# The order of products in the grapher, and mixing stages written out with the root last on ScalarE

## What is computed

```python
h = jnp.concatenate([h, xj], axis=1)
h = gelu(_bn(_pw(h, gc_w, gc_b), ...))          # gc
h = _bn(_pw(h, fc2_w, fc2_b), ...)              # fc2
x = x + ls1 * h                                 # x1
f = gelu(_bn(_pw(x, ffn_w1, ffn_b1), ...))      # ffn1, 64 -> 256 channels
f = _bn(_pw(f, ffn_w2, ffn_b2), ...)            # ffn2, 256 -> 64
x = x + ls2 * f                                 # x2; then relu, 2x2 max pool
```

```python
y = jnp.einsum('bchw,oc->bohw', u_k, conv_w) + conv_b[None, :, None, None]
mu = mean(y over channels); var = mean((y - mu) ** 2 over channels)
t = (y - mu) / jnp.sqrt(var + 1e-5) * ln_w + ln_b; relu(t)
```

## Time and profile before

| | |
|---|---|
| median of 3 runs | 9370.02 us (9359.23 to 9374.55) |
| the profiled execution | 9378.68 us, its span 9376.8 us |
| PE busy in the span | 6280.3 us (67%) |
| DVE (VectorE) busy | 5327.1 us (57%) |
| ACT (ScalarE) busy | 4362.6 us (47%) |
| mean granted TensorE clock | 0.872 |

### The profile page before, as it was taken

The page is one execution under the profiler, slowest core; times in us unless marked ns, Lnnn a source line. Parts: engine busy times, 40 slices in busy tenths (PEclk is TensorE's granted clock), DMA queues, the critical chain, the costliest instruction groups (busy, mean ns, idle before and its releaser), DMA issues. The chain is left out here.

```text
span 9376.8 us, 84057 instructions
## 1 busy us (share of the span) xinstructions
PE 6280.3 (67%) x26092; PEld 3162.9 (34%) x26286; DVE 5327.1 (57%) x5868; ACT 4362.6 (47%) x4790; POOL 3216.9 (34%) x1140
## 2 busy tenths in 40 slices
PE   7895666566666566676566623153998858988787
PEld 5671111111111111224211101142886546764453
DVE  2111888888888788442488666333222233575583
ACT  1223887788888788551488612101001211134445
POOL 0361888788888788000478302000000000000000
PEclk9997898889899888998888867566999978998898
DMA  7558111101210100456300212154657788943343
GB/s 124 140 188 226 19 19 27 54 27 18 36 18 19 63 27 10 134 152 114 94 1 10 65 55 44 32 96 129 103 90 134 164 168 149 233 120 126 117 119 130
DMA packets 1477062, 842.45 MB, mean 90 GB/s; under 512 B 638787, under 2 KB 1406041, under 8 KB 1462953
## 3 DMA queue, kind: packets, MB, share of 16 engines
q1 hardware_dynamic: 1261320, 718.06, 34.0%
q10 hardware_dynamic: 215456, 120.95, 5.5%
HBM read 534.22 MB, written 304.65 MB: 89 GB/s over the span
## 5 line engine op out<-in xcount | busy, mean ns | idle before, releaser
L1016 POOL TENSOR_TENSOR ag_D<-ag_X 128x2048 f32<-128x2048 f32 (+15 forms) x940 | 2909.9, 3111 | 1679.7 <-DMA ag_X<-h 1058.5
L1077 PE MATMUL ag_slot<-ag_S,ag_w 128*128 128x512 bf16 x4768 | 1422.4, 419 | 874.3 <-ACT ag_slot L1046 837.5
L1121 DVE TENSOR_TENSOR ag_J<-ag_J,ag_slot 128x1024 f32<-128x1024 f32 x1240 | 1514.2, 1221 | 279.7 <-PE ag_slot L1077 119.5
L1046 ACT ACTIVATE ag_slot<-ag_D 128x1024 f32<-128x1024 f32 x1280 | 1308.5, 1022 | 674.8 <-DVE ag_J L1128 619.7
L1128 DVE SCALAR_TENSOR_TENSOR ag_J<-ag_slot,ag_J 128x1024 f32<-128x1024 f32 (+14 forms) x1640 | 1539.2, 939 | 144.9 <-DVE ag_J L1121 6.4
L1030 ACT ACTIVATE ag_A<-ag_D 128x2048 f32<-128x2048 f32 x640 | 1212.2, 1894 | 0.1
L1077 PEld LDWEIGHTS ag_slot<-ag_S,ag_w 128*128 128x128 bf16 x4960 | 397.5, 103 | 2264.0 <-ACT ag_slot L1046 1881.9
L1070 PE MATMUL ag_dist<-ag_A,ag_given 128*32 128x512 f32 x5120 | 842.3, 736 | 455.9 <-ACT ag_A L1030 455.6
L255 PE MATMUL dc_ps<-dc_high,dc_w_high 128*128 128x512 f32 (+1 forms) x1056 | 424.6, 402 | 282.7 <-DVE dc_low L68 282.7
L1038 ACT ACTIVATE ag_S<-ag_dist,ag_limit 128x512 bf16<-128x512 f32 x640 | 486.3, 760 | 1.4 <-PE ag_dist L1070 1.4
L269 ACT ACTIVATE dc_out<-dc_ps,shift,scale 128x512 f32<-128x512 f32 (+1 forms) x88 | 67.3, 765 | 817.9 <-PE dc_ps L255 817.9
(11 more groups left out here) (208 smaller groups left out, 9845.4 us busy)
## 6 DMA issues: line engine op xcount, KB each, us to landing
ag_X<-h SPq DMA_DIRECT2D x18, 2048.0 KB, 13.0
xj<-ag_J SPq DMA_DIRECT2D x18, 2048.0 KB, 7.3
c_mul<-gated SPq DMA_DIRECT2D x64, 512.0 KB, 11.6
wa_x<-r SPq DMA_DIRECT2D x128, 256.0 KB, 2.9
u<-wa_x SPq DMA_DIRECT2D x128, 256.0 KB, 2.4
mn_x<-u SPq DMA_DIRECT2D x64, 512.0 KB, 5.3
cpe_band<-in_band SPq DMA_DIRECT2D x16, 1792.0 KB, 8.2
gr_hj<-h SPq DMA_DIRECT2D x168, 128.0 KB, 2.8
```

The lines of the kernel that those rows point to most:

```text
L1016: pool.tensor_tensor(self.tile_part(self.d[u % self.DEPTH][:], u, piece), self.span(g, axis, there, there + hi - lo), self.span(g, axis, l ...
L1046: act.activation(self.slot[v % self.SLOTS][:].rearrange("c b s -> c (b s)"), self.d[u % self.DEPTH][:, h * self.SUB:(h + 1) * self.SUB], A ...
L1077: mm = self.nc.tensor.matmul(self.slot[v % self.SLOTS][:, b, :], self.w[:, weights + 2 * h + b, :], self.s[u % 3][:], start=False, stop=Tr ...
L1121: dve.tensor_tensor(best, best, new, ALU.max).then_inc(self.dve_steps, 1)
```

## The change

In `grapher`, PE issues fc2 of block s-1 right behind ffn1 of block s-2, ahead of gc.

In `mix_norm` the loop is written out in Python over all 16 batches, and the order within a step spreads over more batches: x has three buffers, y four, sq and z two, rep three banks; var has one bank instead of two. A tile's variances go to a quarter of the partitions of `var`, by a product with 32 columns of weights that does not accumulate; the reciprocal of that quarter comes back by a product with 32 rows of weights. One table `sel` takes the place of `gather` and `spread`. Semaphores start at zero (`counted`), and a load signals one semaphore per buffer for both pairs.

```diff
@@ grapher, tensor @@
             for s in range(NB + 3):
                 if there(s - 2):
                     ffn1(s - 2)
+                if there(s - 1):
+                    fc2(s - 1)
                 if there(s):
                     gc(s)
                 if there(s - 3):
                     ffn2(s - 3)
-                if there(s - 1):
-                    fc2(s - 1)
@@ mix_norm @@
+    XR, YR, RR = 3, 4, 3
-        gather = sb("gather", [P, TB, P])
-        spread = sb("spread", [P, TB, P])
+        sel = sb("sel", [P, 32 + P])
...
+        quarter = lambda k: slice(32 * k, 32 * k + 32)
@@ sync @@
+            def load(b):
+                reach(sp, summed, (b - XR + 1) * TB)
...
+            def store(b):
+                sp.wait_ge(relued, (b + 1) * TB)
...
+            for s in range(NB + 5):
+                if there(s):
+                    load(s)
+                if there(s - 5):
+                    store(s - 5)
@@ tensor @@
+            def front(b):
+                pe.wait_ge(loaded[b % XR], 32 * (b // XR + 1))
                 for k, (p, j) in enumerate(tiles):
+                    reach(pe, squared, (b - 1) * TB + k + 1)
+                    mm(acc[k][:], w[:], x[b % XR][p][:, j * BANK:(j + 1) * BANK], start=True, stop=True).then_inc(summed, 1)
+
+            def spread_out(b):
+                reach(pe, dev_made, b)
                 for k in range(TB):
+                    pe.wait_ge(squared, b * TB + k + 1)
+                    mm(var[quarter(k), :], sel[:, 0:32], sq[b % 2][k][:], start=True, stop=True).then_inc(var_summed, 1)
+
+            def back(b):
+                pe.wait_ge(inverted, b + 1)
                 for k in range(TB):
+                    at = b * TB + k
+                    reach(pe, normed, at - RR + 1)
+                    mm(rep[at % RR][:], sel[quarter(k), 32:32 + P], inv[b % 2][quarter(k), :], start=True, stop=True)\
+                        .then_inc(spread_made, 1)
+
+            for s in range(NB + 2):
+                if there(s - 1):
+                    spread_out(s - 1)
+                if there(s):
+                    front(s)
+                if there(s - 2):
+                    back(s - 2)
@@ scalar @@
+            def deviation(b):
+                act.wait_ge(var_summed, (b + 1) * TB)
+                reach(act, inverted, b - 1)
+                act.activation(dev[b % 2][:], var[:], ACT.Sqrt, bias=eps[:, 0:1]).then_inc(dev_made, 1)
...
+            for s in range(NB + 3):
+                if there(s):
+                    front(s)
+                if there(s - 3):
+                    back(s - 3)
+                if there(s):
+                    deviation(s)
@@ vector @@
+            for s in range(NB + 2):
+                if there(s - 1):
+                    invert(s - 1)
+                if there(s - 2):
+                    normalize(s - 2)
```

More of the change, by code:

```diff
@@ L1780, in mix_norm @@
         acc = [ps(f"acc{k}") for k in range(TB)]
[L1781 to L1785, removed]
+        var = ps("var")
+        rep = [ps(f"rep{k}") for k in range(RR)]
+        v = ctx.enter_context(counted(nc, "w_loaded", "w_steps", "bias_mean", "summed", "shifted", "squared", "var_summed",
+                                      "dev_made", "inverted", "spread_made", "normed", "relu_made",
+                                      *[f"loaded_{e}" for e in range(XR)], *[f"stored_{e}" for e in range(2)]))
         (block, w_loaded, w_step, bias_mean, summed, shifted, squared, var_summed, dev_made, inverted, spread_made, normed,
          relued) = v[:13]
[L1788 to L1805, removed]
+        loaded, stored = v[13:13 + XR], v[13 + XR:]
+        there = lambda b: 0 <= b < NB
+        quarter = lambda k: slice(32 * k, 32 * k + 32)
         @block.sync
@@ L1810, in _ @@
                 sp.dma_start(wt[m * C:(m + 1) * C, :], weight).then_inc(w_loaded, 16)
-            sp.dma_start(gather[:], select[0]).then_inc(w_loaded, 16)
-            sp.dma_start(spread[:], select[1]).then_inc(w_loaded, 16)
-            def load(h, e):
+            sp.dma_start(sel[:], select).then_inc(w_loaded, 16)
+            def load(b):
+                reach(sp, summed, (b - XR + 1) * TB)
                 for p in range(PAIRS):
-                    sp.dma_start(x[e][p][:], src[p, :, bass.ds(h * cols, cols)]).then_inc(loaded[e][p], 16)
-            def store(h, e):
-                sp.wait_ge(relued, START + (h + 1) * TB)
+                    sp.dma_start(x[b % XR][p][:], src[p, :, b * cols:(b + 1) * cols]).then_inc(loaded[b % XR], 16)
+            def store(b):
+                sp.wait_ge(relued, (b + 1) * TB)
                 for p in range(PAIRS):
-                    sp.dma_start(dst[p, :, bass.ds(h * cols, cols)], out[e][p][:].rearrange("c j s -> c (j s)"))\
-                      .then_inc(stored[e][p], 16)
-            for e in range(2):
[L1825 to L1836, removed]
+                    sp.dma_start(dst[p, :, b * cols:(b + 1) * cols], out[b % 2][p][:].rearrange("c j s -> c (j s)"))\
+                      .then_inc(stored[b % 2], 16)
+            for s in range(NB + 5):
[3 more added lines that the diff above has]
+                    store(s - 5)
+            for e in range(2):
+                sp.wait_ge(stored[e], 32 * (NB // 2))
         @block.tensor
@@ L1840, in _ @@
             mm = nc.tensor.matmul
-            pe.wait_ge(w_step, START + 5)
+            pe.wait_ge(w_step, 4)
             mm(acc[0][:, 0:1], mean[:], raw("cb"), start=True, stop=True).then_inc(bias_mean, 1)
-            pe.wait_ge(w_step, START + 8)
-            pe.wait_ge(w_loaded, START + 64)
-            def front(h, e, i):
+            pe.wait_ge(w_step, 8)
+            pe.wait_ge(w_loaded, 48)
+            def front(b):
+                pe.wait_ge(loaded[b % XR], 32 * (b // XR + 1))
                 for k, (p, j) in enumerate(tiles):
[L1848 to L1852, removed]
-                for k in range(TB):
-                    pe.wait_ge(squared, START + h * TB + (k + 1))
-                    last = mm(var[e][:], gather[:, k, :], sq[k][:], start=(k == 0), stop=(k == TB - 1))
-                    last.then_inc(var_summed, 1)
@@ L1866, in _, with front @@
+            for s in range(NB + 2):
[5 more added lines that the diff above has]
+                    back(s - 2)
         @block.scalar
         def _(act):
-            act.wait_ge(w_step, START + 8)
-            def front(h, e, i):
+            act.wait_ge(w_step, 8)
+            def front(b):
                 for k in range(TB):
[L1872 to L1879, removed]
@@ L1881, in back @@
-            def back(h, e, i):
-                for k, (p, j) in enumerate(tiles):
[L1883 to L1888, removed]
+                    act.wait_ge(summed, b * TB + k + 1)
+                    reach(act, normed, (b - YR) * TB + k + 1)
@@ new lines, in back @@
+            def back(b):
+                reach(act, stored[b % 2], 32 * (b // 2))
+                for k, (p, j) in enumerate(tiles):
+                    act.wait_ge(normed, b * TB + k + 1)
+                    act.activation(out[b % 2][p][:, j, :], z[b % 2][k][:], ACT.Relu, bias=raw("lb"), scale=raw("lw")).then_inc(relued, 1)
+            for s in range(NB + 3):
[5 more added lines that the diff above has]
+                    deviation(s)
```

52 lines of the change are left out of this document (25 added, 27 removed).

## The result

The changed kernel takes 9006.24 us, the median of 4 runs (9001.72 to 9006.62), the kernel before 9367.6 us in the runs beside them (4 runs, 9359.23 to 9374.55). The ratio is 0.9613, with an interval of 0.9597 to 0.9630. The forecast was 8994, in a range of 8970 to 9066. The profiled execution took 9006.53 us; span against span, 9376.8 became 9004.7, a gain of 372 where the sum said 376. Median against median the gain is 361 us: the profiled execution of before stood 11 us above the median of these four.

The account below looks back on a forecast made before the run. Open waits between engines were taken as the bound: fc2 to ffn1 in grapher, root and reciprocal in mixing. 144 plus 232 us made 376, so 9002.7, less 8.7 to the median: 8994, range 8970 to 9066.

Parts of the forecast that it names:

- 144 (111, 26, 5, 1 and 1): Grapher: us gained in the five stages by moving fc2, at 1.76 us less per step.
- rival (c): Grapher: another limit, loads or VectorE order, gives 6.5 us a step, +70, 9064; whole gain gone, 9138; chance 0.08.
- Rival (b): Mixing: the quarter products do not pack in this order, 10.3 us per batch, +60, 9054; chance 0.06.
- the two at a time taken: Mixing: rep products with 32-row weights taken to run two at a time, 1.72 us per batch.
- Rival (e): Mixing: hardly gains, since a missed wait closes the loop at 15 us, 9226; chance 0.05.
- the 115 of the sum: Mixing: gain per stage, 111.0 first to last root, 0.7 from an earlier first root, 3.1 from the drain.
- 13 x 8.0: Mixing: the 13 root intervals after the third root at ScalarE's 8.0 us per batch, 104 us per stage.
- the grapher's pause is 1.63 us in every step at a granted clock of 0.98 ..., so I take the full clock: Mixing: PE idling 1.3 to 1.9 us per batch was taken to leave the clock full.
- rival (a): Mixing: PE's clock falls; half the time low +52, 9046, all the time +104, 9098; chance 0.14.
- Rival (d): Mixing: instruction fetches for the written-out loop make it slower; 11.8 us per batch needed to decide; chance 0.01.
- a change of shape costs a whole pass: Mixing: three tile-shape changes per batch at 0.59 us each make PE 7.8 us, costing 3 us in all.

Follow-up runs that it names:

- fill_pause: The changed kernel with one more 128x128 product per mixing batch, result unused, in PE's pause before the fourth rep product: 9008.85 us, 0.9604.
- deep: The changed kernel with var between the third and fourth rep products and one more batch in flight, squares left on ScalarE: 9003.58 us, 0.9602.
- changed_again: The changed kernel itself measured once more, as ground for the runs beside it: 9016.86 us, 0.9615 of the kernel before.
- written_out_only: The kernel before with the mixing loop written out in Python, old order and old shapes: 9362.09 us, 0.9986.
- fc2_third: The changed kernel with fc2 behind gc in the grapher, one more change of tile shape per step: 9036.97 us, 0.9633.
- z first: The changed kernel with VectorE's z products of batch s-2 ahead of the reciprocal of batch s-1: 9019.26 us, 0.9615.
- deep_sq_pool: The changed kernel with squares on GpSimd, var between the third and fourth rep products and one more batch in flight: 8959.81 us, 0.9555.

## Why the prediction held, and where its terms were off

- **Grapher**: right in mechanism, and the total is near in part by luck. 5.70 a step for 5.64, fc2 1.05 for 1.0. The five stages, each from its first to its last instruction, became 108.4, 26.5, 8.4, 4.0 and 1.3 us shorter, 149 in all for 144 (111, 26, 5, 1 and 1). So the first level gained less than was counted, and the small ones more: the count left out that ffn1 of block 0 also comes 1.6 to 2.0 us earlier in each of the first three levels. No rival bound came up, rival (c) is out. (The eight passes of 3.60 us in the earlier trace rows are var's, not acc's; the 0.43 holds for both.)
- **Mixing, mechanism**: right. A batch without a dip is 7.95 us for 8.0, set by ScalarE; the root waits for nothing; with the root early or without packing the batches are 9.25 and 10.30, as the same way of counting had it for those two kernels. Rival (b) is out, since var packs four at a time, and rep packs better than the two at a time taken. Rival (e) is out.
- **Mixing, size**: each stage gained 109 us between first acc and last relu, not the 115 of the sum. The term that was mis-sized most is "13 x 8.0": it measured 13 x 8.34 = 108.4, 4.4 us more. The reason is the step "the grapher's pause is 1.63 us in every step at a granted clock of 0.98 ..., so I take the full clock". A pause of 0.77 to 1.1 us per batch did bring the clock to 0.50 at times, and `fill_pause` removed the dips with the pause. So rival (a) is partly there, at 9 us in place of 52. The first of the 13 intervals is long for another reason (8.35 us, and 8.34 in `fill_pause`, which has no dips). And `deep` has as many windows below 1.00, but batches of 7.94 us: only that part of a dip shows which the slack doesn't take. The price varies from execution to execution: the trace of `changed_again` has 8.53 us where the first trace has 8.34.
- **Mixing, start and end**: the second root came 6.75 and the third 7.68 us later (6.5 and 7.3): 0.6 us. The first root came 1.2 us earlier (0.7). The drain measured 11.9 for 10.5: the eight z products, counted without a gap, wait 0.97 and 0.91 us for rep products while the granted clock is 0.50.
- **The start**: the smaller table gave nothing (counted 1 us), because acc waits for x behind it; the way from the last store to the first load is 1.5 us shorter (counted nothing), which I put down to the counters without START; no run has them alone. The two about cancel.
- **Per part**: 147 + 2 x (109 + 1.5) = 368 of the 372 us. The remaining 4 us were not placed. The median came 12 us above the forecast of 8994, 4 of it by the smaller gain. The rest is the 8.7 us that were taken off because the profiled execution of before stood above its median: the one after stands at its own.
- **Rival (d)**: `written_out_only` was 13 us faster, not slower.
- **Luck**: the total is nearer than its parts. The grapher gave 5 us more than counted, and the mixing stages 12 us less.

That a change of shape costs a whole pass, which would have been 3 us in all, is out: it cost 0.15 us in the grapher (`fc2_third`).

## What to carry to other kernels

Where engines take turns in a loop, look first for a product whose input is made right before it in the same step, and put independent work between; price the new step as the busiest engine's own queue, including the round trips inside that queue, such as a PSUM bank that comes free only through another engine. When one engine sets the pace and another stands 0.4 us below it, relieve both in one change: here one alone gave 13 us, the other 10 to 16, and both 57. A short pause on PE in every batch is not free even when hidden, since here it came with dips of the clock; slack, such as one more batch in flight, has to cover them. And look at the end of a stage as well as at its steady batches: z first won 0.18 us a batch and lost 5 us in the drain.

## What the runs showed of the hardware that was not expected

- Pauses of different lengths are not ranked by length: 1.63 us in every 7.40 us left the grapher before at 1.00 from 3820 to 4270 (0.98 over the whole stage), 0.77 to 1.1 us in every 8 us left the mixing at 0.91 with stretches of 2 us at 0.50. The small products alone do not do it: `deep_sq_pool` has them without a pause, and 1.00 from 8432 to 8512. Whether they matter together with a pause was not tested.
- Six passes with 32 rows of weights take 1.13 us, so at least three lie side by side in the array (one at a time they would start 0.43 apart and take 2.7).
- ScalarE's recorded durations drift while it never idles. In `fill_pause` they grow from batch to batch, but the starts of y and sq stay 0.57 apart, so the spacing is the cost, not the duration:

```profile
8480.73 0.95 ACT L1859 ACTIVATE mn_y<-mn_acc,mn_bc 128x512 f32<-128x512 f32 x1
8481.30 0.96 ACT L1861 ACTIVATE mn_sq<-mn_acc,mn_bc 128x512 f32<-128x512 f32 x1
...
8492.66 1.06 ACT L1861 ACTIVATE mn_sq<-mn_acc,mn_bc 128x512 f32<-128x512 f32 x1
```

- GpSimd multiplies a 128x512 tile in about 1.0 us (four in 4.03 in `deep_sq_pool`; spans of that engine are rough), and VectorE's reciprocal beside it keeps its 3.35 us.
